# Two-step products one slot nearer to use, 16 warm-up matmuls, and MLP parts 64 wide in the other column half of TensorE

## What is computed

```
e = stack([tbl_f[ids[:, f]] for f in range(32)], axis=1)        # 1024 x 32 x 16
x0 = xk = e
for W in (W0, W1, W2):                                          # 32 x 32|64 x 64
    xk = relu(einsum('bmd,bhd,mhk->bkd', x0, xk, W))            # 1024 x 64 x 16
    outs.append(sum(xk, axis=2))                                # 1024 x 64
h = concatenate([outs..., dense_ctx], axis=1)                   # 1024 x 208
h = relu(h @ W_top1 + b_top1)                                   # 512
h = relu(h @ W_top2 + b_top2)                                   # 256
y = h @ W_top3                                                  # 1
```

## Time and profile before

| | us |
|---|---|
| time, median of 3 runs (lowest, highest) | 692.79 (692.69, 693.05) |
| the profiled execution, its own time | 687.14 |
| its span, first to last instruction | 685.3 |

### The profile page before, as it was taken

How to read it: one execution, slowest core, us unless ns; L and a number is a source line. 1 busy time by engine, 2 the same in 40 slices (tenths; PEclk the granted TensorE clock), 3 DMA queues, 4 the chain that set the end, 5 groups by cost and what they waited for, 6 DMA issues and landing times.

```text
span 685.3 us, 7935 instructions
## 1 busy us (share of the span) xinstructions
PE 634.0 (93%) x2824; PEld 229.8 (34%) x2824; DVE 509.3 (74%) x343; ACT 312.1 (46%) x521; POOL 444.1 (65%) x346
## 2 busy tenths in 40 slices
PE   2787999999898989999998989899999899979997
PEld 1522333433332323333333333233343233323333
DVE  0046589989888888899887979878998889892210
ACT  1214545454555363645454455536463645621222
POOL 6775557868586767687876868677877665550301
PEclk9999999999999999999999999999999999999999
DMA  4778575857775858667675857585757667530000
GB/s 126 261 272 289 214 258 170 285 197 272 239 260 164 290 188 259 256 222 288 218 280 196 283 191 262 193 304 196 275 194 279 232 211 301 177 125 0 1 0 0
DMA packets 45197, 144.46 MB, mean 211 GB/s; under 512 B 9619, under 2 KB 24085, under 8 KB 32870
## 3 DMA queue, kind: packets, MB, share of 16 engines
q1 hardware_dynamic: 36966, 141.85, 57.3%
q0 software_dynamic: 8192, 2.11, 3.1%
HBM read 139.21 MB, written 4.72 MB: 210 GB/s over the span
## 4 chain that ended last, share of the span: by engine, by line
PE 86%; DVE 5%; issue 4%; ACT 2%; DMA 1%; SPq 1%; POOL 1%; DVEq 0%; POOLq 0%
PE acc L634 61%; PE acc L626 12%; DVE dve_ring L555 4%; PE x_ps L600 3%; PE acc L612 2%; PE sums_ps L659 1%; PE acc L683 1%; DVE z_half L566 1%; PE x_ps L659 1%; PE sums_ps L652 1%; DMA w_sb<-in_w 1%; ACT x_ps L496 1%; PE sums_ps L653 1%; POOL pool_ring L448 1%; PE sums_ps L671 1%
## 5 line engine op out<-in xcount | busy, mean ns | idle before, releaser
L555 DVE TENSOR_TENSOR dve_ring<-x_wide,x_ps 128x1024 f32<-128x1024 f32 (+1 forms) x317 | 482.9, 1589 | 133.1 <-PE acc L634 52.3
L634 PE MATMUL acc<-dve_ring,w_sb 128*64 128x512 f32 x1712 | 507.6, 603 | 28.3 <-DVE dve_ring L555 28.3
L448 POOL TENSOR_TENSOR pool_ring<-x_wide,x_sb 128x1024 f32<-128x1024 f32 x84 | 198.6, 2374 | 154.9 <-PE acc L626 96.8
L436 POOL DMA_INDIRECT gathered<-in_table,idx x256 | 244.4, 955 | 69.6 <-issue 58.7
L634 PEld LDWEIGHTS acc<-dve_ring,w_sb 128*64 128x64 f32 x1712 | 165.4, 139 | 317.1 <-issue 304.4
L626 PE MATMUL acc<-pool_ring,w_sb 128*64 128x512 f32 x336 | 139.8, 593 | 0.0
L612 PE MATMUL acc<-pair_squares,w_sb 128*64 128x512 f32 x256 | 115.7, 592 | 2.4 <-ACT pair_squares L477 2.4
L496 ACT ACTIVATE x_ps<-acc 64x512 f32<-64x512 f32 x128 | 73.0, 570 | 92.6 <-PE acc L634 79.2
L500 ACT ACTIVATE layer_out<-acc 64x512 f32<-64x512 f32 x96 | 56.5, 589 | 64.5 <-PE acc L634 34.4
L505 ACT COPY x_sb<-layer_out 64x512 f32<-64x512 f32 x128 | 79.0, 617 | 3.6
L477 ACT ACTIVATE pair_squares<-x_ps 128x1024 f32<-128x1024 f32 x32 | 32.8, 1024 | 89.8 <-PE sums_ps L600 89.8
(11 more groups left out here) (40 smaller groups left out, 107.9 us busy)
## 6 DMA issues: line engine op xcount, KB each, us to landing
x_wide<-x_rows SPq DMA_DIRECT2D x96, 1024.0 KB, 8.2
x_wide<-x_rows SPq DMA_DIRECT2D x32, 768.0 KB, 5.7
x_wide<-x_rows SPq DMA_DIRECT2D x32, 256.0 KB, 3.0
gathered<-in_table,idx POOLq DMA_INDIRECT x256
x_rows<-gathered SPq DMA_DIRECT2D x32, 128.0 KB
w_sb<-in_w SPq DMA_DIRECT2D x2, 512.0 KB, 5.0
x_rows<-gathered SPq DMA_DIRECT2D x32, 16.0 KB
x_wide<-in_W_top SPq DMA_DIRECT2D x1, 512.0 KB, 4.5
```

Of the source, the lines that this page charges most:

```text
L436: pool.indirect_dma_start(gathered[:, c, j % 2, e * DIM:(e + 1) * DIM], None, table, bass.IndirectOffsetOnAxis(ap=idx[:, unit, e:e + 1], a ...
L448: nc.gpsimd.tensor_tensor(pool_ring[:, c], x0_step(c, j, layer, 2 * d, 2).rearrange("p (s n) -> p s n", n=COLS), x_sb[:, layer - 1, c, :]. ...
L555: nc.vector.tensor_tensor(dve_ring[:, c, slot:slot + width, :], x0_step(c, j, layer, i, width).rearrange("p (s n) -> p s n", n=COLS), x_ps ...
L634: done = nc.tensor.matmul(a, w, dve_ring[:, c, n % DVE_RING + i - at, :], start=first, stop=last)
```

## The change

- `dve_groups`: every product on VectorE covers two steps; none covers four.
- `LEAD` is 5 instead of 6: products of VectorE stand one slot nearer to their steps, where the slot of layer 2's bound (18.5) does not decide.
- `WARM_UP` is 16 instead of 34.
- The MLP is cut into 8 + 4 + 1 parts for each chunk. A part gives 64 outputs and uses one column half of TensorE. `mlp_plan` writes down where each part goes: in 24 matmuls of the first chunk one stands beside each step of a thread that has the other half free; the rest stands behind the last step, in pairs of one part for either half, and the last few parts alone. Four PSUM banks serve the parts instead of three.
- The MLP's loads on SyncE's queue now wait for thread 0's unit 14 alone and stand ahead of the last x0 block instead of behind it. The first part waits in return for the products of thread 1's unit 14, as its `h1` lies over that unit's x0.

The core of the diff:

```diff
-WARM_UP = 34
+WARM_UP = 16
-LEAD = 6
+LEAD = 5
-MLP_PARTS = [(layer, j) for layer, width in ((1, H1), (2, H2)) for j in range(width // P)] + [(3, 0)]
+MLP_PARTS = [(layer, j) for layer, width in ((1, H1), (2, H2)) for j in range(width // HK)] + [(3, 0)]
+MLP_STEPS = {1: 2, 2: H1 // P, 3: H2 // P}
 def dve_groups(c, j, layer):
-    groups = []
-    for i in range(0, STEPS, 2):
...
-            groups[-1] = (i - 2, 4)
-        else:
-            groups.append((i, 2))
-    return groups
+    return [(i, 2) for i in range(0, STEPS, 2) if not by_pool(c, j, layer, i)]
+def mlp_plan():
+    first = [begin(c, UNITS - 1) + STEPS for c in range(THREADS)]
+    last = [begin(c, UNITS) for c in range(THREADS)]
+    layer1, layer2 = range(H1 // HK), range(H1 // HK, (H1 + H2) // HK)
+    end = len(MLP_PARTS) - 1
+    runs = [(0, first[0], [(0, i) for i in layer1[0:2]]),
+            (1, first[1], [(0, i) for i in layer1[2:4]]),
+            (0, last[0], [(0, i) for i in layer1[4:8]] + [(0, i) for i in layer2[0:2]]),
+            (0, last[1], [(0, layer2[2])] + [(1, i) for i in layer1[0::2]] + [(2, i) for i in layer1[0::2]]
+             + [(1, i) for i in layer2[0::2]] + [(0, end)] + [(2, i) for i in layer2[0::2]] + [(1, end), (2, end)]),
+            (1, last[1], [(0, layer2[3])] + [(1, i) for i in layer1[1::2]] + [(2, i) for i in layer1[1::2]]
+             + [(1, i) for i in layer2[1::2]] + [(2, i) for i in layer2[1::2]])]
+    for half, at, parts in runs:
+        for n, i in parts:
+            steps = MLP_STEPS[MLP_PARTS[i][0]]
+            one = MLP_CHUNKS[n][1] / COLS
+            plan.append((at, one, half, n, i))
+            at += steps * one
 def pe_order():
-    for n, first in enumerate((begin(0, UNITS - 1) + STEPS, begin(1, UNITS - 1) + STEPS, begin(1, UNITS) + 1)):
-        works += [(first + 1.5 * i + 0.7, "mlp", n, i, 0, 0) for i in range(len(MLP_PARTS))]
+    for number, (at, one, half, n, i) in enumerate(mlp_plan()):
+        works += [(at + one * k, "mlp", number, half, n, i, k) for k in range(MLP_STEPS[MLP_PARTS[i][0]])]
 def sp_order():
-    works.append((begin(1, UNITS - 2) + UNIT_SLOTS, "mlp", 0, 0, 0))
+    works.append((begin(0, UNITS - 1) + 1, "mlp", 0, 0, 0))
-        mlp_banks = [sums_ps[:, 0, :], sums_ps[:, 1, :], x_ps[:, BANK[1, 0], :]]
+        mlp_banks = [sums_ps[:, 0, :], sums_ps[:, 1, :], x_ps[:, BANK[1, 0], :], x_ps[:, BANK[2, 0], :]]
-                    for thread in range(THREADS):
-                        block_read(thread, UNITS - 2, 1)
+                    block_read(0, UNITS - 2, 1)
+            def mlp_step(number, half, n, i, k):
+                cols, w_cols = slice(first, first + rows), slice(j * HK, (j + 1) * HK)
+                bank = mlp_bank(n, i)[out_half(half), 0:rows]
...
+                done = nc.tensor.matmul(bank, w, x, start=(k == 0), stop=(k == MLP_STEPS[layer] - 1))
```

More of the change, by code:

```diff
@@ L116, in dve_groups, with mlp_done_order @@
 def dve_groups(c, j, layer):
-    groups = []
-    for i in range(0, STEPS, 2):
[L119 to L122, removed]
-            groups[-1] = (i - 2, 4)
-        else:
-            groups.append((i, 2))
-    return groups
+    return [(i, 2) for i in range(0, STEPS, 2) if not by_pool(c, j, layer, i)]
[11 more added lines that the diff above has]
+             + [(1, i) for i in layer2[1::2]] + [(2, i) for i in layer2[1::2]])]
+    plan = []
+    for half, at, parts in runs:
[4 more added lines that the diff above has]
+            at += steps * one
+    return sorted(plan)
+def mlp_done_order():
+    ends = [(at + one * (MLP_STEPS[MLP_PARTS[i][0]] - 1), at, n, i, half) for at, one, half, n, i in mlp_plan()]
+    return [(end + 1.2, n, i, half) for end, at, n, i, half in sorted(ends)]
 def in_order(works):
@@ L167, in act_order @@
     works += [(z_slot(layer, tile) + 1, "place", layer, tile, 0) for layer in range(LAYERS) for tile in range(TILES)]
-    for n, first in enumerate((begin(0, UNITS - 1) + STEPS, begin(1, UNITS - 1) + STEPS, begin(1, UNITS) + 3.5)):
-        works += [(first + 1.5 * i + 1.7, "mlp", n, i, 0) for i in range(len(MLP_PARTS))]
+    works += [(at, "mlp", half, n, i) for at, n, i, half in mlp_done_order()]
     return in_order(works)
@@ L539, in _ @@
                 else:
[L540 removed]
+                    hidden(*at)
         @block.vector
@@ L643, in mlp_product @@
                     pe.wait_ge(mlp_loaded, MLP_LOADS)
                     pe.wait_ge(squares_made, 3 * THREADS * UNITS)
+                    pe.wait_ge(dve_made[1], dve_before(1, UNITS - 2, 2, STEPS))
+                    pe.wait_ge(pool_made[1], pool_before(1, UNITS - 2, 2, STEPS))
                     pe.wait_ge(dve_made[0], dve_before(0, UNITS - 1, 2))
-                if i == 0:
-                    for l in range(LAYERS):
-                        pe.wait_ge(z_made[l], 2 * (first + rows) // P)
@@ L666, in mlp_product @@
-                last.then_inc(mlp_done, 1)
+                if number == len(mlp_banks) - 1 and k == 0:
+                    pe.wait_ge(dve_made[0], dve_before(0, UNITS - 1, 2, STEPS))
+                if number >= len(mlp_banks) and k == 0:
+                    pe.wait_ge(hidden_made, mlp_count(*mlp_starts[number - len(mlp_banks)]))
+                if layer == 1:
+                    if k == 0:
+                        for l in range(LAYERS):
+                            pe.wait_ge(z_made[l], 2 * (first + rows) // P)
+                    rows_in = slice(0, REST if k else P)
+                    w, x = wt1[rows_in, k, w_cols], features[rows_in, k, cols]
+                elif layer == 2:
+                    for before in (2 * k, 2 * k + 1):
+                        pe.wait_ge(hidden_made, mlp_count(n, MLP_PARTS.index((1, before))))
+                    w, x = wt2[:, k, w_cols], h1[:, k, cols]
+                else:
+                    for before in (2 * k, 2 * k + 1):
+                        pe.wait_ge(hidden_made, mlp_count(n, MLP_PARTS.index((2, before))))
+                    w, x, bank = wt3[:, k:k + 1], h2[:, k, cols], bank[0:1, :]
```

52 lines of the change are left out of this document (21 added, 31 removed).

## The result

The changed kernel takes 630.45 us (median of 4 runs, 629.0 to 633.92) against 692.74 of the kernel before in the same comparison; the ratio is 0.9117, interval 0.9072 to 0.9161. It is 62 us faster, and lies in the range (628 to 660), 10.5 us under the forecast of 641.

A forecast was written before the change was run, and what follows sets the result against it. Bound: TensorE waiting 2.3 us a unit for VectorE, whose long products hold the line. −28 (units), −7 (start) and −17 (tail) make −52: 687.14 to 635.1, plus 5.65 to the median, 641 us; range 628 to 660.

The forecast's parts named there:

- The bound and the head of line: 13 units, 91 to 566 us: TensorE waits 2.3 us a unit behind four-step products on VectorE; two-step ones give −28.
- the prediction's walk: VectorE's work list between the points where `x_ps` opens it: 2 and 2.5 us to spare before layer 2.
- Splitting is nearly free: VectorE, 13 units: two queued two-step products cost 2.26 us against 2.28 for a long one; 32.3 us a unit.
- Start: Before the 13 units: fewer warm-up matmuls, shorter first products and earlier loads give −7 in all (−3 to −9).
- The warm-up's −4.1: Before the first `sums`: 16 matmuls take 3.68 us where 34 take 7.81, and nothing later holds these sums: −4.1.
- The last term: Thread 1's second `sums` to thread 0's third: 21 slots and one `sums`, 19.3 of the 20.2 us that pass: −1.
- Tail: From thread 1's last step 0 of layer 1 to the end: 75.4 us become 58.1, −17 (−13 to −20).
- The rival by which parts don't pair: MLP in the tail: parts don't run beside the other half, 37.8 us more, 679 us; chance 0.06.
- carrying 5.65 us from the profiled execution to the median: Last step of the sum: median 692.79 lies 5.65 above the profiled 687.14, so 635.1 becomes 640.8.
- The renamed wait: Rival, 13 units: TensorE waits for VectorE at another place; half of the 28 kept, 655 us (648 to 660); chance 0.24.
- Lockstep: Rival, 13 units: each two-step product waits 0.33 us for ring places, 43.5 us a unit, 759 us; chance 0.03.
- The prediction's sign that products would now wait mostly for the ring: 13 units, VectorE: if the forecast holds, the products' idle time before them is now mostly behind the ring.

## Why the prediction was right, point by point

*The bound and the head of line.* Distances, not busy shares, gave 2.3 us of waits a unit, and that is what came back: 36.6 to 34.20. The busy row hid a part: TensorE's idle time before in that stretch, 475.0 − 455.57 = 19.4 us, is well below the 31.3 regained. The mechanism holds, but the line was held longer than the prediction had it: in seven units the last product ahead of thread 0's layer 2 waited for thread 1's step 3 of the next layer, four slots behind the step 15 of the prediction. And **the prediction gave `LEAD` the wrong role**: it costed the edit at nothing and looked only for lost cover. Alone it is worth 24.5 us of the 13 units, because it moves one product of each unit behind thread 0's; beside two-step products it is worth nothing (444.62 with either). In the prediction's walk two steps of thread 1 move behind; in the order of work that stands ahead of it, four do. The term was −28 for −31.3, beyond its bound of −30: the twelfth that I let stay was not there, and a unit without waits is 34.20 us, not 34.28.

*Splitting is nearly free.* The size was right: 1.13 us a product, 32.3 forecast and 421.3 / 13 = 32.4 measured of VectorE in a unit. But the prediction set two distances, 2.26, against one recorded length, 2.28. Two queued long products of before:

```profile
309.48 4.48 DVE L555 TENSOR_TENSOR dve_ring<-x_wide,x_ps 128x2048 f32<-128x2048 f32 x2
```

They start 4.48 − 2.28 = 2.20 us apart, so a split costs 2.26 − 2.20 = 0.06 us of VectorE, some 5.5 us for the 92, and it did not show because VectorE had that to spare. The Trainium skill, "VectorE: DVE Perf Modes", section "The TRN2 errata — SBUF-src ops pay a fixed extra latency per instruction", has one large tile pay that latency once and many small ones each time. The trace agrees in kind, with 0.06 us for each further instruction; the 0.15 that the prediction worked out by that rule took recorded lengths for distances, and the earlier trace rows do not speak against the rule.

*Start.* −7.3 against −7, from two terms that erred in opposite ways. The warm-up's −4.1 was right at equal clock and showed as −1.9. The rest was −5.4 for −3.1, and here the difference is the clock too: before has stretches of 0.50 at about 36.0 to 39.4 and 56.5 to 59.9, after one, 51.2 to 54.7. One such stretch less is 1.7 us (half of 3.4), and −3.7 are left beside −3.1; the changed kernel with 34 warm-up matmuls has two stretches, as before has, and takes 61.96 us here, −3.7. Of these, −2.1 are the two waits for first products, 3.72 us each in before and 2.66 in after, as forecast. The last term was mis-sized: from thread 1's second `sums` to thread 0's third are 18.4 us in after, where the prediction had 19.3.

*Tail.* −17.8 against −17. MLP matmuls beside steps cost 0.6 us at most, the loads' wait went, and the reliefs behind the last step were near the 4 us added. The rival by which parts don't pair falls: steps and MLP matmuls start 10 ns apart. The Trainium skill, "TensorE: Matmul & The Clock Gate", section "Part 3: Packing small matmuls — row/col tiling", has weights loaded beside running matmuls only when the rows differ. The trace disagrees: all rows are the same here, each pass loads its weights (2133 loads beside 2134 passes in the 13 units), and one half's passes follow at 0.43 us as the pairs of both halves do, with one load or two. That the pairing would give nothing by that rule was the prediction's own conclusion, and no run bears it out. One slip: from thread 1's last step 0 of layer 1, at 571.27, to its last step, which starts at 601.32 and takes a slot, are 30.9 us or 36 slots, not 37; the rest took 26.8 us where the sum had 26.3.

*The step that failed* is the last one of the sum: **carrying 5.65 us from the profiled execution to the median**. After has no such gap (630.75 against 630.45), and these 5.65 are over half of the 10.5 us by which the forecast was off. The gap is no constant of a run; it goes with TensorE's clock. Three stretches in the 13 units of before:

```profile
179.50:182.70 3.20, 3.20 (x10) 0.50 0.48 141
363.80:367.00 3.20, 3.20 (x10) 0.50 0.50 159
438.90:442.10 3.20, 2.81 (x8) 0.50 0.22 44
```

They are at half of the clock, 1.2 of 2.4 GHz. Each begins within about half a us of a wait's end (waits of 1.79, 2.92 and 2.91 us that end at 179.04, 363.18 and 439.29), and after has none in its 13 units. How many there are differs from run to run: of twenty further runs of before, six have a mean granted clock of 0.988 and spans of 685.3 to 687.7 us, six have 0.983 and 687.0 to 690.8, seven 0.978 and 691.6 to 695.5; one at 0.993 has 686.6. From 0.988 to 0.978 the clock alone takes 0.010 × 690 = 6.9 us, and the middle spans differ by 8.4. The medians of before in the three comparisons are 688.84, 690.87 and 693.29. The execution that I read, 685.3 at 0.988, was one of the lucky ones; the clock of the three runs behind 692.79 is not on record. The MLP change alone, put to the same question, answers half of it: its median is 0.7 us above its profiled execution, so the 5.65 is no constant; but its four runs all have 0.985 and lie within 1.1 us, though its 13 units wait as before's do (475.73 us). So waits don't scatter the runs by themselves, and why some executions meet more stretches at half clock stays open.

*The rivals.* The renamed wait did not come; TensorE waits nowhere in the 13 units. Lockstep did not come either: no wait on the ring is left. The prediction's sign that products would now wait mostly for the ring was wrong too: what is left, 23.3 us, stands before the first products of a layer 2.

## What to carry to other kernels

In a list that is executed in order, look for the one instruction that stands just ahead of the critical one, and ask what it waits for: ten split products, or one of each unit moved by a slot, did some three quarters of what splitting all did. Count waits from distances between like instructions, since a busy share hides a half that stands still, and set distances against distances: a recorded length is not one. And before a profiled time is carried to a median, look at whether the granted clock of the other runs is the same; the stretches at half clock stand near waits.

## What the runs showed of the hardware

VectorE's products overlap by 0.08 us when queued: 1.21 recorded, 1.13 apart, ten in a row; twice as long, 2.28 recorded, 2.20 apart. Two halves thus take 0.06 us more than one whole. Matmuls with equal rows and different columns, each with its own weights, run side by side: starts 10 ns apart, 0.43 us a pass with a partner or without. Some waits of TensorE of 1.8 to 3.7 us had a stretch at half clock of 3.4 us or more beginning near their end, which costs about 1.7 us or more beside the idle time, and others had not: of two waits of 2.92 us in before, the one that ends at 363.18 had, the one that ends at 218.51 had not; of two of 2.66 in after, the one that ends at 51.44 had, the one that ends at 32.36 had not.
